# A fused attention and expert block: the second norm's shift moved into DRAM, the query constants and a transposition reordered

## The chip, the cores and the metric

The kernel runs on one core of a Trainium2 chip. The metric is the device time of one launch in microseconds; the time given for a kernel is the median over its runs.

## The reference

One adaptive-norm block over x of shape 4 x 2048 x 512 (8192 rows). Six modulation vectors per batch come from a conditioning input: shift, scale and gate for the attention (sa, ca, ga) and for the experts (sb, cb, gb).

```python
h = layernorm(x) * (1 + ca) + sa
x = x + ga * attention(h)          # segments of 128 rows, one head of width 512, plus a global part per segment
h = layernorm(x) * (1 + cb) + sb   # the second norm
x = x + gb * experts(h)            # top-1 routing to 16 experts, 512 slots each, 512 -> 2048 -> 512 with relu
```

The router takes softmax(h @ Wg + bg), the largest score of each row and its rank among the rows of the same expert; a row beyond slot 511 of its expert is dropped. In the attention the products of query and key are folded into one matrix (M = Wq' Wk), so a row's score has besides h M h' a constant per row, the query constant, that comes from the biases: the dot product of the normalised row with a vector vc per batch, plus a constant.

## The kernel before, in words

A prologue folds the weights and makes the modulation rows. Then 16 groups of 512 rows (four tiles of 128 rows, called segments here) run through a software pipeline, and at last 16 experts run one after the other. All fp32 products are made from a high and a low part in three matmuls (`split3`, L326 to L330).

In iteration i of the pipeline every engine's program (five programs, written out by hand and tied by semaphores) works on several groups at once: group i is projected (G tiles, U rows), group i-1 has its softmax and attention product, its residual and its second norm, group i-2 has its normalised rows h2 transposed for the router, and group i-3 is routed and scattered into the slot table. Each engine works strictly in the order of its own program.

TensorE (L687 to L775), for group i: G tile 0, transposes of the logit parts, G tile 1, transposes of h2 of group i-2 (L715), G tile 2, transposes of prob of group i-1 (L726), G tile 3, the attention product of group i-1 (L744, which reads pt_hi, pt_lo, u_hi, u_lo), U of group i (L754), the router's logit parts of group i-2 (L761), the transposes of the normalised rows xn of group i+1 (`transpose_xn`, L598), and the scores of group i (L773). The PSUM banks 0 to 3 (`big`) are used again and again: the transposes of xn for k = 0, 1, 2 write the banks from which VectorE takes u_lo(0), u_lo(1), u_lo(2), and wait for the semaphore u_split (L596); the scores go to bank 3 and wait for u_lo(3) (L770).

VectorE (L1339 to L1402): the softmax constants of group i-1, the router's logits, the probabilities, the statistics of the first norm of group i+1 (`stats1`), pt_lo (L1364), the router's slots (`route_slots`), h and the residual xr of group i-1 (L1377, L1381), the statistics of the second norm, then for group i the low parts u_lo (L1399) of the four U tiles. Between the second and the third of these stands `query_const` (L1265): four scalar_tensor_tensor instructions (L1271), one per segment, which multiply the rows of x with vc and sum them up, and a small one (L1275). Their elementwise result goes to `qc_junk`, which lies over the tile `prob`. Then come the low parts ht_lo of group i+1 (L1217).

ScalarE (L1001 to L1060): the exponentials, gt (`add_u`, L965), h2t (L1034, a Copy out of PSUM), pt_hi (L1039), u_hi(0) to u_hi(2) (L1009), the normalised rows of segments 0 to 2 of group i-1 (`normalise2`, L1016), u_hi(3), segment 3, then `modulate` for group i+1 (L957) and the logit parts (L1013).

GpSimd (L1594 to L1616): `normalise1` of group i+1 (L1558, L1561, four L1568), the scatter of group i-3 into the slot table (four indirect DMAs, L1590), the inverse root of the second norm, and then for each segment of group i-1 the product with 1 + cb (L1611) and the sum with sb (L1615), both in place in h2. For the last group VectorE does this for three of the segments (L1388 to L1393).

SP (L434 to L454) issues the loads and stores: x of group i+2, the global rows, xr of group i (a second load of x), then for group i-1 the store of the residual (L452), and the store of h2 into the DRAM tensor h_rows (L454), from which the experts later gather their rows. It waits for the semaphore before each of them, and everything behind it in the queue waits too.

```python
for s in range(GS):
    if s == 2:
        query_const(i)
    dve.wait_ge(u_hi_done, 4 * n + s + 1)
    dve.tensor_tensor(u_lo[:, s, :], big[s][:, :], u_hi[:, s, :].bitcast(F32), ALU.subtract) \
        .then_inc(u_split, 1)
```

Of the kernel before, what the change touches and what calls it, by code (L numbers as in the profile page):

```python
# [60 lines left out]
def build_block(nc, x, wq, bq, wk, bk, wv, bv, wo, bo, wg, bg, w1, b1, w2, b2, cond, wmod, out):  # L61
# [90 lines left out]
    bk_cols = keep("bk_cols", [P, KC, NBATCH], F32)  # L152
    q_const = keep("q_const", [P, 4], F32)
# [26 lines left out]
    logit_parts, = over(cursor[0], ("logit_parts", [P, ROWS], F32))  # L180
# [28 lines left out]
    qc_junk = prob[:].rearrange("p s t -> p (s t)")  # L209
# [32 lines left out]
    def sem(name):  # L242
# [35 lines left out]
    x2_ready, ln2_step, ln2_ready, ln2_rstd, xn2_done, h2_scaled, h2_ready = (sem(k) for k in (  # L278
        "x2_ready", "ln2_step", "ln2_ready", "ln2_rstd", "xn2_done", "h2_scaled", "h2_ready"))
    last_scaled = sem("last_scaled")  # L280
    x2_stored = [sem(f"x2_stored{i}") for i in range(2)]
    h2_stored = [sem(f"h2_stored{i}") for i in range(2)]
# [36 lines left out]
    def batch_of(g):  # L319
        return g.n // GPB  # L320

    def t1_bank(g, k):

        return t1_last if k == KC - 1 and not (isinstance(g.n, int) and g.n == 0) else big[k]

    def split3(pe, o, a_hi, a_lo, b_hi, b_lo, start, stop):  # L326
# [9 lines left out]
    (MCH, SCT, BCOL, FIRST4, WOT, UCOL, MCOL, VCH, HGT, LATE4, GROWS, GGT, SG, BROW, PGT, TG, B1T,  # L336
     PRO_END) = (0, 4, 5, 6, 7, 11, 12, 13, 17, 18, 19, 20, 21, 22, 23, 24, 25, 26)
# [24 lines left out]
    def _(sp):  # L362
        def w_rows(w):
            return w.rearrange("(c p) n -> p c n", p=P)

        def group_rows(rows, g):
            return rows[bass.ds(g.n * ROWS, ROWS), :].rearrange("(s p) d -> p s d", p=P)
# [66 lines left out]
        def iteration(i, cur, prev, load2):  # L434
# [5 lines left out]
            if cur:  # L440
# [7 lines left out]
                sp.dma_start(xr[i.par][:], group_rows(x_rows, i)).then_inc(xr_in[i.par], 16)  # L448
            if prev:
# [3 lines left out]
                sp.wait_ge(h2_ready, 4 * g.n + 4)  # L453
                sp.dma_start(group_rows(h2_dram, g), h2[g.par][:]).then_inc(h2_stored[g.par], 16)  # L454
# [36 lines left out]
        sp.wait_ge(h2_ready, 4 * NG)  # L491
# [32 lines left out]
    def _(pe):  # L524
# [130 lines left out]
        g_tile(Group(0, 0), 3)  # L655
        pe.wait_ge(gsum_prob, 1)
# [30 lines left out]
        def iteration(i, cur, prev, prev2, nxt, prev3):  # L687
# [59 lines left out]
            if cur:  # L747
                for s in range(GS):
# [7 lines left out]
                    last.then_inc(u_full, 1)  # L756
            if prev2:
# [6 lines left out]
            if cur and not g_tiles:  # L764
                pe.wait_ge(pro_evac, PRO_END)
            if nxt:
                transpose_xn(i.plus(1), False)
# [151 lines left out]
    def _(act):  # L919
# [76 lines left out]
        add_u(Group(0, 0), 3)  # L996
        copy_out(PGT, pg_t[:], pro_bank(PGT)[0:NSEG, 0:NSEG])
# [3 lines left out]
        def iteration(i, cur, prev, prev2, nxt, prev3):  # L1001
# [51 lines left out]
            if cur:  # L1053
                empty_u(3)
            if prev:
                normalise2(3)
# [654 lines left out]
```

## Time and profile before

| | |
|---|---|
| median of 3 runs | 1887.14 us (1886.38 to 1889.94) |
| the profiled execution, its own time | 1889.13 us |
| its span in the profile | 1887.4 us |
| granted clock of TensorE, mean | 0.984 |
| TensorE matmul busy | 1796.1 us (95%) |
| VectorE busy | 1225.6 us (65%) |
| ScalarE busy | 822.7 us (44%) |
| GpSimd busy | 870.3 us (46%) |
| DMA | 270.77 MB, mean 143 GB/s |

The prologue lasts until about 90 us, the 16 groups until about 640 us, the routing of the last groups and the first gather until about 690 us, and the experts from there to the end. Busy time of TensorE is what its matmuls cover; a wait shows as idle time ahead of the instruction that had to wait, with the name of what ended it.

### The profile page before, as it was taken

The numbers are of one execution on the slowest core, as the hardware profiler recorded it, in microseconds if no ns is written. First come the engines' busy times: TensorE is split into PE (matmuls) and PEld (weight loads), VectorE is DVE, ScalarE is ACT, GpSimd is POOL, SyncE is SP. The second block draws the span as 40 slices with busy tenths as digits, with TensorE's granted clock in tenths as the row PEclk, the third lists the DMA queues.
The fourth block names the chain that finished last, engine by engine and source line by source line (L and its number), as shares of the span: only waits on it lengthen the run. The fifth ranks groups of instructions, "written<-read, shape, count | busy, mean of one in ns | idle before, by whom it ended". The sixth has DMA issues, their size and how long they took to land.

```text
span 1887.4 us, 28151 instructions
## 1 busy us (share of the span) xinstructions
PE 1796.1 (95%) x9137; PEld 1486.9 (79%) x9138; DVE 1225.6 (65%) x1882; ACT 822.7 (44%) x1322; POOL 870.3 (46%) x709
## 2 busy tenths in 40 slices
PE   8999999999999549999999999999998999999998
PEld 3677787787787437888888888888888988888886
DVE  4568888888887753556554554537658886455762
ACT  2544554544554322433433343335545564334541
POOL 2145655656665441334343432416636757233632
PEclk9999999999999879999999999999999999999999
DMA  8322432342242524343535434345545455434622
GB/s 276 140 92 90 138 131 90 119 149 89 103 166 89 178 68 160 130 142 125 190 134 180 146 123 144 116 157 190 175 142 205 164 210 182 155 123 156 215 88 67
DMA packets 137915, 270.77 MB, mean 143 GB/s; under 512 B 17633, under 2 KB 18221, under 8 KB 137862
## 3 DMA queue, kind: packets, MB, share of 16 engines
q1 hardware_dynamic: 115338, 221.27, 33.6%
q0 software_dynamic: 22528, 48.86, 8.1%
q8 instruction: 29, 0.48, 0.1%
q14 instruction: 20, 0.16, 0.0%
HBM read 237.71 MB, written 50.72 MB: 153 GB/s over the span
## 4 chain that ended last, share of the span: by engine, by line
PE 77%; DVE 14%; issue 4%; ACT 3%; DMA 1%; POOL 0%; DVEq 0%; POOLq 0%; ACTq 0%; SPq 0%
PE bank L328 23%; PE bank L330 23%; PE bank L329 23%; PE bank L773 3%; DVE prob L1271 2%; DVE h L1377 2%; DVE xr L1381 2%; DVE stats L1156 2%; PE bank L715 1%; DVE u_lo L1399 1%; PE bank L816 1%; PE bank L598 1%; PE bank L536 1%; PE bank L587 1%; DVE h_lo L1438 0%
## 5 line engine op out<-in xcount | busy, mean ns | idle before, releaser
L1438 DVE TENSOR_TENSOR h_lo<-h_f,h_hi 128x512 fp32r<-128x512 f32 x256 | 221.3, 885 | 363.4 <-ACT h_f L1090 363.2
L1089 ACT ACTIVATE h_hi<-bank,b_col 128x512 fp32r<-128x512 f32 x256 | 176.4, 689 | 599.6 <-PE bank L330 582.1
L328 PE MATMUL bank<-bt_hi,w_hi 128*128 128x512 f32 (+4 forms) x1024 | 360.3, 352 | 8.4 <-DVE w_lo L1409 5.6
L330 PE MATMUL bank<-bt_hi,w_lo 128*128 128x512 f32 (+4 forms) x1024 | 359.4, 351 | 0.0
L329 PE MATMUL bank<-bt_lo,w_hi 128*128 128x512 f32 (+4 forms) x1024 | 359.4, 351 | 0.0
L328 PE MATMUL bank<-w_hi,h_hi 128*128 128x512 f32 x832 | 326.9, 393 | 3.3 <-DVE h_lo L1438 2.5
L329 PE MATMUL bank<-w_lo,h_hi 128*128 128x512 f32 x832 | 325.4, 391 | 0.0
L330 PE MATMUL bank<-w_hi,h_lo 128*128 128x512 f32 x832 | 324.9, 391 | 0.0
L328 PEld LDWEIGHTS bank<-bt_hi,w_hi 128*128 128x128 f32 x1024 | 194.7, 190 | 33.6 <-issue 9.6
L329 PEld LDWEIGHTS bank<-bt_lo,w_hi 128*128 128x128 f32 x1024 | 194.7, 190 | 21.0
L330 PEld LDWEIGHTS bank<-bt_hi,w_lo 128*128 128x128 f32 x1024 | 194.7, 190 | 20.3
L1634 POOL DMA_INDIRECT gb_rows<-mod_rows,tok_g x64 | 79.5, 1243 | 277.4 <-DVE tok_g L1515 221.6
L328 PEld LDWEIGHTS bank<-w_hi,h_hi 128*128 128x128 f32 x832 | 157.0, 189 | 36.4 <-issue 5.0
L330 PEld LDWEIGHTS bank<-w_hi,h_lo 128*128 128x128 f32 x832 | 156.9, 189 | 33.0
L329 PEld LDWEIGHTS bank<-w_lo,h_hi 128*128 128x128 f32 x832 | 156.9, 189 | 31.2
L1634 POOL DMA_INDIRECT xh<-h_rows,tok_h x64 | 87.1, 1361 | 201.2 <-DVE tok_h L1497 177.8
L1430 DVE TENSOR_TENSOR w_lo<-raw,w_hi 128x2048 fp32r<-128x2048 f32 x64 | 153.1, 2393 | 41.0 <-ACT w_hi L1079 40.9
L1090 ACT ACTIVATE h_f<-bank,b_col 128x512 f32<-128x512 f32 x256 | 174.3, 681 | 0.0
L1409 DVE TENSOR_TENSOR w_lo<-raw,w_hi 128x2048 fp32r<-128x2048 f32 x64 | 152.8, 2388 | 2.2
L1660 POOL TENSOR_TENSOR yo<-yo,gb_rows 128x512 f32<-128x512 f32 x60 | 96.1, 1602 | 107.0 <-DVE yo L1459 105.6
L1079 ACT ACTIVATE w_hi<-raw 128x2048 fp32r<-128x2048 f32 x64 | 122.6, 1916 | 0.0
L1665 POOL DMA_INDIRECT out_dram<-yo,tok_x x64 | 79.8, 1247 | 80.7 <-POOL yo L1662 53.9
(265 smaller groups left out, 3220.4 us busy)
## 6 DMA issues: line engine op xcount, KB each, us to landing
raw<-in_L_ffn_W_dram SPq DMA_DIRECT2D x128, 1024.0 KB, 5.5
xa<-in_L_attn_x_dram SPq DMA_DIRECT2D x16, 1024.0 KB, 5.3
xr<-in_L_attn_x_dram SPq DMA_DIRECT2D x16, 1024.0 KB, 8.1
out_dram<-xr SPq DMA_DIRECT2D x16, 1024.0 KB, 10.2
h_rows<-h SPq DMA_DIRECT2D x16, 1024.0 KB, 4.3
b_bc<-in_L_ffn_b_dram SPq DMA_DIRECT2D x16, 256.0 KB, 6.2
wm_a<-in_L_wmod_dram SPq DMA_DIRECT2D x2, 1024.0 KB, 11.1
wm_b<-in_L_wmod_dram SPq DMA_DIRECT2D x2, 1024.0 KB, 11.2
```

What stands on the lines that cost most here:

```text
L328: pe.matmul(o, a_hi, b_hi, start=start, stop=False)
L329: pe.matmul(o, a_hi, b_lo, start=False, stop=False)
L330: return pe.matmul(o, a_lo, b_hi, start=False, stop=stop)
L1079: act.activation(w2_hi[b % 2][:], raw[2 * (b % 2) + 1][:], ACT.Copy).then_inc(w2_hi_done, 1)
L1089: act.activation(h1_hi[b % 2][:, j, :], h_bank[j][:, :], ACT.Relu, bias=bias)
L1090: act.activation(h1_f[:, j, :], h_bank[j][:, :], ACT.Relu, bias=bias).then_inc(relu_done, 1)
L1409: dve.tensor_tensor(w1_lo[b % 2][:], raw[2 * (b % 2)][:], w1_hi[b % 2][:].bitcast(F32), ALU.subtract) \
L1430: dve.tensor_tensor(w2_lo[b % 2][:], raw[2 * (b % 2) + 1][:], w2_hi[b % 2][:].bitcast(F32), ALU.subtract) \
L1438: dve.tensor_tensor(h1_lo[b % 2][:, j, :], h1_f[:, j, :], h1_hi[b % 2][:, j, :].bitcast(F32), ALU.subtract) \
L1634: pool.indirect_dma_start(out=rows[:, j, :], out_offset=None, in_=source, in_offset=bass.IndirectOffsetOnAxis(tokens[:, j:j + 1], 0), boun ...
L1660: pool.tensor_tensor(yo[:, j, :], yo[:, j, :], gb_rows[:, j, :], ALU.mult).then_inc(y_scaled, 1)
L1665: pool.indirect_dma_start(out=out_rows, out_offset=bass.IndirectOffsetOnAxis(tok_x[:, j:j + 1], 0), in_=yo[:, j, :], in_offset=None, bound ...
```

## The change

- The second norm's shift sb is no longer added by GpSimd (L1615) or VectorE (L1393). SP writes it into h_rows for each group, broadcast from the table `sb_tab`, after the load of xr; for group 0 it first waits for the three late tables. GpSimd then, when the four segments are scaled and that store has landed (new semaphores `shift_stored`), issues one DMA that adds h2 to what is in h_rows. SP's store of h2 and its wait for h2_ready go.
- The router needs the shifted rows, so ScalarE adds the shift as it evicts the transposed rows (Identity with a bias per partition, `sb_col`, instead of Copy). `sb_col` takes the place of sc_t in memory and is made in the prologue by four small transposes (SCOL) and one copy.
- On VectorE the query rows of segments 0 to 2 stand after `stats1` and ahead of pt_lo, that of segment 3 ahead of u_lo(0), and the small instruction L1275 behind u_lo(0). `qc_junk` has memory of its own.
- On TensorE `transpose_xn` stands ahead of the logit parts, directly after U.
- On ScalarE `modulate` of the next group stands ahead of `normalise2(3)`.

```diff
@@ sync @@
                 sp.dma_start(xr[i.par][:], group_rows(x_rows, i)).then_inc(xr_in[i.par], 16)
+
+                if isinstance(i.n, int) and i.n == 0:
+                    sp.wait_ge(late_tab_in, 48)
+                shift = sb_tab[:, bass.ds(batch_of(i), 1), :].to_broadcast([P, GS, D])
+                sp.dma_start(group_rows(h2_dram, i), shift).then_inc(shift_stored[i.par], 16)
...
                 sp.dma_start(group_rows(out_rows, g), xr[g.par][:]).then_inc(x2_stored[g.par], 16)
-                sp.wait_ge(h2_ready, 4 * g.n + 4)
-                sp.dma_start(group_rows(h2_dram, g), h2[g.par][:]).then_inc(h2_stored[g.par], 16)
...
-        sp.wait_ge(h2_ready, 4 * NG)
@@ tensor @@
         g_tile(Group(0, 0), 3)
+        bank_free(SCOL)
+        for k in range(KC):
+            last = pe.transpose(pro_bank(SCOL)[:, k * NBATCH:(k + 1) * NBATCH], modr[:, SB, chunk(k)],
+                                ident[0:NBATCH, 0:NBATCH])
+        product(SCOL, last)
...
                     last.then_inc(u_full, 1)
+            if cur and not g_tiles:
+                pe.wait_ge(pro_evac, PRO_END)
+            if nxt:
+                transpose_xn(i.plus(1), False)
             if prev2:
                 pe.wait_ge(h2t_done, 4 * p2.n + 4)
...
                 last.then_inc(parts_full, 1)
-            if cur and not g_tiles:
-                pe.wait_ge(pro_evac, PRO_END)
-            if nxt:
-                transpose_xn(i.plus(1), False)
@@ scalar @@
+        copy_out(SCOL, sb_col[:].rearrange("p k b -> p (k b)"), pro_bank(SCOL)[:, 0:KC * NBATCH])
...
-                    act.activation(h2t[:, k, :], big[(k + 2) % 4][:, :], ACT.Copy).then_inc(h2t_done, 1)
+                    act.activation(h2t[:, k, :], big[(k + 2) % 4][:, :], ACT.Identity,
+                                   bias=sb_col[:, k, bass.ds(batch_of(p2), 1)]).then_inc(h2t_done, 1)
...
+            if nxt:
+                modulate(i.plus(1))
             if prev:
                 normalise2(3)
-            if nxt:
-                modulate(i.plus(1))
@@ vector @@
             if nxt:
                 stats1(i.plus(1))
+            if cur:
+
+                for s in range(GS - 1):
+                    query_row(i, s)
...
-                    dve.tensor_tensor(rows, rows, cb_tab[:, batch_of(p1), :], ALU.mult).then_inc(last_scaled, 1)
-                    dve.wait_ge(last_scaled, s + 1)
-                    dve.tensor_tensor(rows, rows, sb_tab[:, batch_of(p1), :], ALU.add).then_inc(h2_ready, 1)
+                    dve.tensor_tensor(rows, rows, cb_tab[:, batch_of(p1), :], ALU.mult).then_inc(h2_ready, 1)
             if cur:
+                query_row(i, GS - 1)
                 for s in range(GS):
-                    if s == 2:
-                        query_const(i)
                     dve.wait_ge(u_hi_done, 4 * n + s + 1)
                     dve.tensor_tensor(u_lo[:, s, :], big[s][:, :], u_hi[:, s, :].bitcast(F32), ALU.subtract) \
                         .then_inc(u_split, 1)
+                    if s == 0:
+                        query_const(i)
@@ gpsimd @@
                     pool.tensor_tensor(rows, rows, cb_tab[:, bass.ds(b, 1), :].rearrange("p b d -> p (b d)"), ALU.mult) \
-                        .then_inc(h2_scaled, 1)
-                    pool.wait_ge(h2_scaled, 4 * p1.n + s + 1 - first_seg)
-                    stand_alone(pool, pool_passed)
-                    pool.tensor_tensor(rows, rows, sb_tab[:, bass.ds(b, 1), :].rearrange("p b d -> p (b d)"), ALU.add) \
                         .then_inc(h2_ready, 1)
+                pool.wait_ge(h2_ready, 4 * p1.n + 4)
+                pool.wait_ge(shift_stored[p1.par], 16 * (p1.half + 1))
+                stand_alone(pool, pool_passed)
+                pool.dma_start(group_rows(h2_dram, p1), h2[p1.par][:], accum_op=ALU.add).then_inc(h2_stored[p1.par], 16)
```

`query_row` is the body of the old `query_const` for one segment, and `query_const` keeps the small instruction alone.

## Rows read from the trace of the kernel before

**Rows 1.** Stages: us, PE, PEld, DVE, ACT, POOL busy, clock, DMA, GB/s.

```profile
197.00:589.00 392.00, 383.42 (x2134) 307.91 (x2133) 339.97 (x790) 194.28 (x380) 239.44 (x219) 1.00 0.35 121
690.00:1280.00 590.00, 586.54 (x2727) 499.46 (x2728) 304.66 (x285) 225.13 (x311) 200.10 (x158) 1.00 0.42 144
```

**Rows 2.** TensorE waits, 88 to 640 us: total us, times, longest us.

```profile
PE bank L598 <- DVE u_lo L1399: 9.0, 12, 1.2
PE bank L715 <- POOL h L1615: 2.4, 1, 2.4
PE bank L773 <- DVE u_lo L1399: 2.1, 1, 2.1
...
PE bank L328 <- DVE ht_lo L1217: 1.1, 2, 0.7
```

**Rows 3.** TensorE timeline: start us, us, what [idle before, what ended it].

```profile
228.67 1.09 PE L598 MATMUL bank<-ident,xa 128*128 128x128 f32 x8 [0.59 <-DVE u_lo L1399]
...
549.91 0.39 PE L330 MATMUL bank<-v_hi,ht_lo 128*128 128x512 f32 x1
...
551.22 1.09 PE L598 MATMUL bank<-ident,xa 128*128 128x128 f32 x8
552.89 1.09 PE L598 MATMUL bank<-ident,xa 128*128 128x128 f32 x8 [0.57 <-DVE u_lo L1399]
...
588.73 1.09 PE L598 MATMUL bank<-ident,xa 128*128 128x128 f32 x8 [0.60 <-DVE u_lo L1399]
```

**Rows 4.** Timeline of VectorE at the end of the same period.

```profile
549.38 1.69 DVE L1271 SCALAR_TENSOR_TENSOR prob<-xa,vc_tab 128x512 f32<-128x512 f32 x1
...
551.22 1.02 DVE L1275 TENSOR_SCALAR per_tok<-per_tok,qc_bc 128x4 f32<-128x4 f32 x1
552.15 1.28 DVE L1399 TENSOR_TENSOR u_lo<-bank,u_hi 128x512 fp32r<-128x512 f32 x2
```

**Rows 5.** Timeline of all engines around pt_lo in that period.

```profile
531.15 0.16 DVE L1163 TENSOR_SCALAR per_tok<-mv 128x4 f32<-128x4 f32 x1
...
531.39 1.02 POOL L1558 TENSOR_TENSOR per_tok<-per_tok,half_neg 128x4 f32<-128x4 f32 x1 [5.45 <-DVE per_tok L1163]
...
532.52 0.69 ACT L965 ACTIVATE gt<-bank,u_col 128x512 f32<-128x512 f32 x1 [2.08 <-PE bank L330]
...
532.90 3.06 POOL L1568 TENSOR_SCALAR xa<-xa,per_tok 128x512 f32<-128x512 f32 x4 [0.21 <-POOL per_tok L1561]
...
533.73 0.69 DVE L1364 TENSOR_TENSOR pt_lo<-bank,pt_hi 128x512 fp32r<-128x512 f32 x1 [2.42 <-ACT pt_hi L1039]
...
535.52 0.39 PE L328 MATMUL bank<-u_hi,pt_hi 128*128 128x512 f32 x1
```

**Rows 6.** Timeline of ScalarE, that period and group 15.

```profile
548.11 2.22 ACT L1016 ACTIVATE h<-xr,per_tok 128x512 f32<-128x512 f32 x3
...
621.93 0.60 ACT L1009 ACTIVATE u_hi<-bank 128x512 fp32r<-128x512 f32 x1
```

**Rows 7.** Timeline of VectorE at the start of a period.

```profile
518.57 4.76 DVE L1217 TENSOR_TENSOR ht_lo<-ht,ht_hi 128x512 fp32r<-128x512 f32 x3 [0.30 <-ACT ht L957]
```

**Rows 8.** One line's instructions, GpSimd's shift: ns min/median/max.

```profile
L1615 POOL TENSOR_TENSOR h<-h,sb_tab x61: 1261/1497/1783, 120.6 to 653.0; 128x512 f32<-128x512 f32 x61
```

**Rows 9.** Timeline of GpSimd, one DMA of the scatter.

```profile
542.58 1.02 POOL L1590 DMA_INDIRECT slot_table<-pay,slot_i  x1 [0.30 <-issue]
```

**Rows 10.** DMA issues: count, KB each, median us to landing.

```profile
h_rows<-h SPq DMA_DIRECT2D x16, 1024.0 KB, 4.3
```

**Rows 11.** Timeline of the last groups, all engines.

```profile
625.02 3.81 PE L773 MATMUL bank<-ht,gt 128*128 128x128 f32 x32 [2.13 <-DVE u_lo L1399]
...
651.23 1.60 POOL L1611 TENSOR_TENSOR h<-h,cb_tab 128x512 f32<-128x512 f32 x1 [3.14 <-ACT h L1016]
...
653.41 1.63 DVE L1393 TENSOR_TENSOR h<-h,sb_tab 128x512 f32<-128x512 f32 x1
```

**Rows 12.** Timeline of VectorE in group 0, beside normalise1.

```profile
84.80 1.14 DVE L1271 SCALAR_TENSOR_TENSOR prob<-xa,vc_tab 128x512 f32<-128x512 f32 x1
```

More of the change, by code:

```diff
@@ L152, in build_block @@
     bk_cols = keep("bk_cols", [P, KC, NBATCH], F32)
+    sb_col = sc_t
     q_const = keep("q_const", [P, 4], F32)
@@ L179, in build_block @@
     prob, pt_hi, pt_lo = over(r_p, ("prob", seg_sq, F32), ("pt_hi", seg_sq, F32R), ("pt_lo", seg_sq, F32R))
-    logit_parts, = over(cursor[0], ("logit_parts", [P, ROWS], F32))
+    logit_parts, qc_junk = over(cursor[0], ("logit_parts", [P, ROWS], F32), ("qc_junk", [P, D], F32))
     batch_rows = [P, NBATCH, D]
@@ L208, in build_block @@
     m_f.append(m_f3)
-    qc_junk = prob[:].rearrange("p s t -> p (s t)")
     QCS2 = [QC, QCS]
@@ L277, in build_block @@
         "pt_full", "pt_hi_done", "pt_split", "av_full", "av_taken"))
-    x2_ready, ln2_step, ln2_ready, ln2_rstd, xn2_done, h2_scaled, h2_ready = (sem(k) for k in (
-        "x2_ready", "ln2_step", "ln2_ready", "ln2_rstd", "xn2_done", "h2_scaled", "h2_ready"))
-    last_scaled = sem("last_scaled")
+    x2_ready, ln2_step, ln2_ready, ln2_rstd, xn2_done, h2_ready = (sem(k) for k in (
+        "x2_ready", "ln2_step", "ln2_ready", "ln2_rstd", "xn2_done", "h2_ready"))
     x2_stored = [sem(f"x2_stored{i}") for i in range(2)]
+    shift_stored = [sem(f"shift_stored{i}") for i in range(2)]
     h2_stored = [sem(f"h2_stored{i}") for i in range(2)]
@@ L320, in batch_of, with group_rows @@
         return g.n // GPB
+    def group_rows(rows, g):
+        return rows[bass.ds(g.n * ROWS, ROWS), :].rearrange("(s p) d -> p s d", p=P)
     def t1_bank(g, k):
@@ L330, in split3 @@
         return pe.matmul(o, a_lo, b_hi, start=False, stop=stop)
-    (MCH, SCT, BCOL, FIRST4, WOT, UCOL, MCOL, VCH, HGT, LATE4, GROWS, GGT, SG, BROW, PGT, TG, B1T,
-     PRO_END) = (0, 4, 5, 6, 7, 11, 12, 13, 17, 18, 19, 20, 21, 22, 23, 24, 25, 26)
+    (MCH, SCT, BCOL, FIRST4, WOT, UCOL, MCOL, VCH, HGT, LATE4, GROWS, GGT, SG, BROW, SCOL, PGT, TG,
+     B1T, PRO_END) = (0, 4, 5, 6, 7, 11, 12, 13, 17, 18, 19, 20, 21, 22, 23, 24, 25, 26, 27)
     def pro_bank(q):
@@ L364, in w_rows @@
             return w.rearrange("(c p) n -> p c n", p=P)
-        def group_rows(rows, g):
-            return rows[bass.ds(g.n * ROWS, ROWS), :].rearrange("(s p) d -> p s d", p=P)
         def load_x(g):
@@ L1263, in _, with query_row @@
         dve.wait_ge(made, POOL_MADE)
-        def query_const(g):
-            b = batch_of(g)
-            for s in range(GS):
-                if s > 0:
-                    dve.wait_ge(qc_raw, 4 * g.n + s)
-                dve.scalar_tensor_tensor(out=qc_junk, in0=xa[g.par][:, s, :], scalar=1.0,
-                                         in1=vc_tab[:, bass.ds(b, 1), :].rearrange("p b d -> p (b d)"), op0=ALU.mult,
-                                         op1=ALU.mult, accum_out=QRAW[:, s:s + 1]).then_inc(qc_raw, 1)
+        def query_row(g, s):
+            wait_past(dve, qc_raw, 4 * g.n + s)
+            dve.scalar_tensor_tensor(out=qc_junk[:], in0=xa[g.par][:, s, :], scalar=1.0,
+                                     in1=vc_tab[:, bass.ds(batch_of(g), 1), :].rearrange("p b d -> p (b d)"),
+                                     op0=ALU.mult, op1=ALU.mult, accum_out=QRAW[:, s:s + 1]).then_inc(qc_raw, 1)
+        def query_const(g):
             dve.wait_ge(qc_raw, 4 * g.n + 4)
-            dve.tensor_scalar(QCS2[g.par], QRAW, qc_bc[:, bass.ds(b, 1)], SCALE, ALU.add, ALU.mult) \
+            dve.tensor_scalar(QCS2[g.par], QRAW, qc_bc[:, bass.ds(batch_of(g), 1)], SCALE, ALU.add, ALU.mult) \
                 .then_inc(qc_ready, 1)
```

## The prediction

> **What bounds the kernel now.** I read the busy time by stage first, then TensorE's waits, then the timeline of one period. In the router-and-attention stage (197 to 589 us) TensorE is busy 383.4 of 392 us, VectorE 340.0 and GpSimd 239.4; in the first experts (690 to 1280 us) TensorE is busy 586.5 of 590 [rows 1]. So the experts, which the change does not touch, have nothing to give, and in the first stage there are only the seconds that TensorE stands still. The list of its waits names them: 9.0 us in 12 waits of the transposes of xn (L598) for VectorE's u_lo (L1399), 2.1 of the scores (L773) for the same, 2.4 of the transposes of h2 (L715) for GpSimd's shift (L1615), 1.1 of a first product for ht_lo [rows 2]. The clock is granted in full there (1.00) [rows 1], so nothing is to be had from it.
>
> How the 9.0 us come about is to be seen in one period. U ends at 550.14 (its last matmul starts at 549.91; they follow each other every 0.23 us), the partial logits of L761 take the time up to 551.22, where eight transposes begin, and the other eight start at 552.89 after 0.57 us of idling [rows 3]. They write bank 2, which u_lo(2) must have left. VectorE reaches it at 552.15, since between u_lo(1) and u_lo(2) stand the four query rows (the last of them takes 1.69 us instead of 0.69) and the small L1275 with 1.02 us [rows 4]. From pt_lo at 533.73 VectorE has had no pause worth the name; the pause lies ahead of it: 2.42 us, from the end of stats1 (531.31) to pt_hi [rows 5]. There are 12 such waits of up to 1.2 us [rows 2], one per period of 36.0 us (228.67 to 588.73 is ten periods [rows 3]).
>
> **The change part by part.**
> (a) Query rows 0 to 2 move ahead of pt_lo, and L1275 behind u_lo(0). Three rows at 0.73 us from start to start are 2.2 us, the pause is 2.42 [rows 5]. Cover: the pause. If it were gone, pt_lo has some 0.9 us to spare: it ends at 534.42, and the first attention product starts at 535.52, its weight load a little before [rows 5]. After statistics there remain: row 3 (0.73), u_lo(0) (0.68), L1275 (between 0.2 and the 1.02 of its row), u_lo(1), u_lo(2). Statistics end at about 546.0 (row 3's 549.38 [rows 4] less three rows of 0.73 and two u_lo of 0.6). That puts the end of u_lo(1) at about 549.3 and of u_lo(2) at 550.0 at the latest, instead of 552.8. TensorE, which now goes to the transposes directly after U (550.14), wants u_lo(2) 1.1 us later, after eight of them, at 551.3. The wait goes entirely.
>
> (b) The transposes go before L761. The work is the same; its order matters for what is late next. Scores need u_lo(3), which needs u_hi(3); ScalarE evicts that only after three rows of normalise2 (548.11 + 2.22 = 550.33) and 0.60 us of its own (as in group 15) [rows 6], so 550.93, and u_lo(3) ends at 551.7. Scores start at 550.14 + 2.18 (16 transposes, twice 1.09) + 1.08 (L761, from U's end to 551.22) = 553.4 [rows 3]. Margin 1.7 us. For the next group modulate starts at once, as normalise2(3) now stands behind it: ht_lo(0) is there about 3 us after U's end, wanted 6.8 us after it. Today the last three ht_lo take 4.76 us beside GpSimd's multiply and add [rows 7]; that gets better with fewer of them. So (a) and (b) together: -9.0 us, and of the 1.1 us for ht_lo in the second group all, since ScalarE reaches modulate one normalise2 (0.74) earlier: -1.1.
>
> (c) GpSimd's four adds of 1.50 us (median) go [rows 8]: 6.0 us per group, off the path except at the end. In their place it waits for the multiplies and the shift store, and issues a 1 MB accumulating store. The trace has no such store; the nearest row is an indirect one of 128 rows at 1.02 us [rows 9], so 512 rows lie between 1.0 and 4 x 1.3 = 5.3 us of issue. I take 5.3, as nearest by rows moved. Queued behind it: normalise1, scatter and the inverse root of the second norm. Cover: GpSimd idles (392 - 239.4) / 10.9 periods = 14.0 us per period [rows 1], and gets 6.0 more. Cost 0; it would begin to bind at 20 us an issue. Landing: unknown, between the 4.3 us of the plain store [rows 10] and several times that; the buffer is overwritten two groups later, some 50 us on, so 0.
>
> (d) SP: the shift store (16 x 1 MB) stands behind xr's load and before the out store, the h2 store leaves, and with it the wait for h2_ready, behind which the next x load was queued. The new wait for the three tables stands in group 0 ahead of the x load for group 3, which waits for transposes anyhow. About 34 MB more traffic in 530 us is 63 GB/s on top of 121, at a DMA share of 0.35 [rows 1]: 0.
>
> (e) h2t with a bias: Identity with a bias from PSUM takes 0.69 (L965) [rows 5] where a Copy takes 0.60 [rows 6], so up to +0.4 us on ScalarE for four. It stands before a wait of 2 us for the next tile: 0 in the loop, 0.4 once at the end, counted in (f).
>
> (f) The last groups, where TensorE waits for others. Group 15's scores wait 2.1 us for u_lo(3); u_hi(3) is out at 621.93 + 0.60 = 622.53 [rows 6], so they can start at about 623.3 instead of 625.02 [rows 11]: -1.7. The 2.4 us that L715 then waits for GpSimd's add [rows 2] mostly lie beside the softmax that starts from the same scores; bounds of the pair 0 and 4.5, I take 1.7. Then the scaling of group 15: three multiplies and adds on VectorE and one of each on GpSimd, alternating, end at 655.04 and TensorE stands idle for it. Without adds the last is GpSimd's multiply, 651.23 + 1.60 = 652.83: -2.2 [rows 11]. All that follows (router, slot table, first gather) hangs on it.
>
> (g) Prologue: four small transposes and a copy more, bound 0.7 us; against it, rows and normalise1 of group 1 collide less or more, bound 0.5. Net 0.
>
> Sum: 9.0 + 1.1 + 1.7 + 2.2 = 14.0 us. The profiled execution took 1889.13 (span 1887.4, 1.7 around it), so 1875.1 for it; it is 2.0 above the median of 1887.14. On the median: 1873.1.
>
> **Rivals.**
> 1. The query rows collide with GpSimd in their new place. For it: the rows read two tiles of SBUF, and beside normalise1 such a row took 1.14 us once, instead of 0.69 [rows 12]; in the pause stand L1558 (1.02 us) and the first of four steps of L1568 (3.06 / 4 = 0.77 each) [rows 5]. If row 1 waits for L1558 and row 2 for one L1568, pt_lo starts at about 535.4, 1.7 late, of which 0.9 is free; TensorE then stalls 0.1 to 0.8 us per period, say 0.5 x 13 = 6.5. Time 1879.6. Against it: three rows colliding by 0.45 each would cost 1.35, half a microsecond beyond the margin at most.
> The Trainium skill (SBUF — State Buffer, Who interferes with whom) says that a VectorE instruction with two SBUF inputs contends with a GpSimd instruction that reads SBUF, and that whoever comes first holds the shared pair for its whole instruction; by that rule this rival is the expected course, and the row of 1.69 us agrees with it.
> 2. The same place, but at today's worst price: a row beside GpSimd costs 1.8 us (the last one does today, 1.69). Three are 5.4 in a pause of 2.4, so pt_lo is 3.0 late, 2.1 beyond its margin, against 0.8 saved: +1.3 x 13 = 17 us, less 5.0 of the other terms: slower, 1899. It decides from 1.7 us of delay per period on. Against it: 1.69 belongs to a two-input instruction of 1.3 to 1.7 us on GpSimd, and here stand ones of 0.77 and 1.02.
> 3. The wait only changes its place: scores wait for u_lo(3) (ScalarE late through the inverse root, or GpSimd held by the accumulating store), or the transposes still wait. Then of 14.0 only (f) and a little more is left: about 5, 1882. Margins of 1.3 and 1.7 us speak against it.
>
> **Numbers.** Forecast 0.62, rival 1 0.20, rival 3 0.11, rival 2 0.07. A difference within 0.2% (3.8 us) can't be told from none. Forecast, rival 1 and half or more of rival 3 are faster: 0.86; the rest of 3: 0.07; rival 2: 0.07. Range: below, the pair in (f) at 4.5 and 1 us elsewhere (18 saved, 1869); above, rival 1 and most of 3, 1882.
>
> **What the profile after would show.** Waits of L598 for u_lo gone, and none of L773, L328 for pt_lo or for h (L1377) in their place; the period 35.2 us (36.0 - 0.8); VectorE's pause before pt_lo under 0.5 us; ht_lo nearer 0.7 than today's 4.76 / 3 = 1.6; GpSimd's DMA issue of at most 5 us; first gather about 14 us earlier; experts unchanged from there. It is wrong if the rows before pt_lo span over 3.3 us, if GpSimd's issue reaches 15 us or more, or if the experts' part changes by more than 2 us.

## The result and the profile after

The changed kernel takes 1865.41 us (median of 5 runs, 1863.25 to 1868.66), the kernel before beside it 1889.65 (5 runs, 1886.38 to 1890.42). The ratio is 0.9875, 95% interval 0.9863 to 0.9886: 24 us less, where 14 were forecast, and below the range's lower end of 1869. The profiled execution took 1863.25 us; its span is 1861.6, against 1887.4 before. It is the fastest of the five, 2.2 us below their median, so what the trace gains (25.8 us) is a little more than what the medians do (24.2).

The stages after, in the columns of [rows 1], each shifted by what had been gained by then:

```profile
190.00:573.00 383.00, 383.00 (x2142) 311.88 (x2151) 300.73 (x791) 199.49 (x383) 192.00 (x187) 1.00 0.55 155
672.00:1262.00 590.00, 589.87 (x2756) 503.30 (x2755) 309.09 (x287) 230.68 (x317) 205.56 (x160) 1.00 0.42 145
```

In the attention loop TensorE never stands still in the records any more (383.00 of 383). The second line answers to the second of [rows 1]: TensorE is busy 589.87 us where it had been busy 586.54. That stage was to have nothing to give. It gave, and this is the largest part of the miss.

TensorE's waits after, 88 to 640 us, beside [rows 2]:

```profile
PE bank L723 <- POOL h L1624: 10.2, 1, 10.2
PE bank L723 <- ACT prob L1031: 1.8, 1, 1.8
PE bank L332 <- DVE pt_lo L1378: 1.7, 1, 1.7
...
PE bank L781 <- DVE u_lo L1410: 0.5, 1, 0.5
```

The 12 waits of the transposes for u_lo are gone, and so are those for ht_lo. What is left lies in the last two groups. The 10.2 is the pause ahead of the last h2 transposes, which in the kernel before (12.7 us for L1393) fell just behind 640 us. The scores of group 15 wait 0.5 instead of 2.1.

Two periods of TensorE's timeline, beside [rows 3]:

```profile
500.52 1.91 PE L601 MATMUL bank<-ident,xa 128*128 128x128 f32 x16
502.36 1.07 PE L773 MATMUL bank<-h2t,wg_s 128*32 128x512 f32 x8
503.35 3.84 PE L781 MATMUL bank<-ht,gt 128*128 128x128 f32 x32
...
535.54 1.91 PE L601 MATMUL bank<-ident,xa 128*128 128x128 f32 x16
```

The period is 35.02 us here. The sixteen transposes now run as one block, and the scores follow the logit parts without a gap.

VectorE and GpSimd ahead of pt_lo, beside [rows 5]:

```profile
516.25 0.17 DVE L1173 TENSOR_SCALAR per_tok<-mv 128x4 f32<-128x4 f32 x1
516.36 0.69 DVE L1278 SCALAR_TENSOR_TENSOR qc_junk<-xa,vc_tab 128x512 f32<-128x512 f32 x1
516.50 1.43 POOL L1571 TENSOR_TENSOR per_tok<-per_tok,half_neg 128x4 f32<-128x4 f32 x1 [5.25 <-DVE per_tok L1173]
...
517.09 0.69 DVE L1278 SCALAR_TENSOR_TENSOR qc_junk<-xa,vc_tab 128x512 f32<-128x512 f32 x1
...
517.83 0.69 DVE L1278 SCALAR_TENSOR_TENSOR qc_junk<-xa,vc_tab 128x512 f32<-128x512 f32 x1
518.01 0.56 POOL L1574 TENSOR_TENSOR per_tok<-per_tok 128x4 f32<-128x4 f32 x1
...
519.13 0.69 DVE L1378 TENSOR_TENSOR pt_lo<-bank,pt_hi 128x512 fp32r<-128x512 f32 x1 [0.61 <-ACT pt_hi L1049]
```

Each query row keeps its 0.69 us and pt_lo still has 0.61 us of pause before it. The collision costs GpSimd instead: its small L1571 takes 1.43 where it took 1.02 [rows 5], and nobody waits for that. The Trainium skill (SBUF — State Buffer, Who interferes with whom) has a VectorE instruction with two SBUF inputs contend with a GpSimd instruction that reads SBUF, and says that the order of issue decides who blocks. The trace agrees for the first row: it starts at 516.36 and keeps its time, GpSimd's instruction starts at 516.50 and loses. The second row does not fit so simply: it starts at 517.09, while L1571 is still running (until 517.93), and keeps its 0.69 us all the same.

The new store (one line's instructions, ns min/median/max) and the DMA issues (us from issue to landing):

```profile
L1629 POOL DMA_DIRECT2D h_rows<-h x16: 1361/1431/1571, 126.2 to 635.5; - x16
```

```profile
h_rows<-h POOLq DMA_DIRECT2D x16, 1024.0 KB, 9.5
```

Issuing costs GpSimd 1.43 us for 512 rows, near the lower bound of 1.0 from [rows 9] and far from the 5.3 taken. It lands after 9.5 us, the plain store of [rows 10] after 4.3.

**Where the time went.** Landmarks of TensorE in the two profiled executions: first scores 90.39 and 87.56 us, those of group 3 193.79 and 188.11, of group 14 589.66 and 573.40, of group 15 625.02 and 607.26; last h2 transposes 655.10 and 634.18; first gathered rows 685.86 and 665.57; the next expert's 768.59 and 743.76; end of span 1887.4 and 1861.6. The differences between successive marks are the gain by stage:

| Stage | gain, us | forecast |
|---|---|---|
| prologue | 2.8 | 0 |
| groups 0 to 14 (14 periods) | 2.9 + 10.6 = 13.4 | 10.1 |
| group 15, tail, router | 1.5 + 3.2 - 0.6 = 4.0 | 3.9 |
| first expert | 4.5 | 0 |
| all other experts | 1.0 | 0 |
| sum | 25.8 | 14.0 |

(The sum is that of the unrounded marks.) So three things want an explanation: 3.3 us more in the loop, 4.5 in the first expert, and 2.8 in the prologue.

### The profile page after: what moved, and what is told of

Same layout as the page of the kernel before. It is cut to its first block, busy times and chain, and to the rows that moved or that the text cites. A ratio compares the mean times of both kernels' runs of the same rounds, so it can differ in the third digit from the quotient of the medians.

```text
span 1861.6 us, 28129 instructions
## 1 busy us (share of the span) xinstructions
PE 1787.6 (96%) x9125; PEld 1486.2 (80%) x9142; DVE 1170.0 (63%) x1879; ACT 828.2 (44%) x1323; POOL 803.4 (43%) x664
## 3 DMA queue, kind: packets, MB, share of 16 engines
HBM read 237.71 MB, written 67.49 MB: 164 GB/s over the span
## 4 chain that ended last, share of the span: by engine, by line
PE 91%; DVE 2%; issue 2%; ACT 2%; POOL 1%; DMA 1%; POOLq 0%; DVEq 0%; ACTq 0%; SPq 0%
PE bank L332 27%; PE bank L334 26%; PE bank L333 26%; PE bank L781 3%; PE bank L723 2%; PE bank L601 1%; PE bank L824 1%; PE bank L590 1%; PE bank L539 1%; PE bank L773 1%; PE bank L753 1%; POOL yo L1675 0%; DMA out_dram<-yo,tok_x 0%; DVE h_lo L1451 0%; PE bank L734 0%
## 5 line engine op out<-in xcount | busy, mean ns | idle before, releaser
L334 PEld LDWEIGHTS bank<-w_hi,h_lo 128*128 128x128 f32 x832 | 156.4, 188 | 32.9
L1571 POOL TENSOR_TENSOR per_tok<-per_tok,half_neg 128x4 f32<-128x4 f32 (+1 forms) x33 | 45.6, 1382 | 167.3 <-DVE per_tok L1173 167.3
## 6 DMA issues: line engine op xcount, KB each, us to landing
wm_a<-in_L_wmod_dram SPq DMA_DIRECT2D x2, 1024.0 KB, 10.6
```

The costliest lines, as they stand in the source:

```text
L334: return pe.matmul(o, a_lo, b_hi, start=False, stop=stop)
```

## The experiments

There were ten runs, each with the kernel before beside it on the same chip; c1 and c6 repeat the two kernels, the other eight are new ones. To tell the parts apart they are called rows (VectorE's query rows and L1275 moved), transposes (ahead of the logit parts), modulation (ahead of the last normalisation) and shift (added in DRAM). The period is the distance between the scores of group 3 and group 14, divided by 11. c5 and c10 follow further down.

| Kernel | rows | transp. | modul. | shift | us | ratio (95%) | period |
|---|---|---|---|---|---|---|---|
| c1 | - | - | - | - | 1888.99 | 1.0005 (0.9995 to 1.0014) | 35.97 |
| c8 | yes | - | - | - | 1894.82 | 1.0028 (1.0018 to 1.0038) | 36.12 |
| c2 | yes | yes | yes | - | 1884.29 | 0.9979 (0.9970 to 0.9988) | 35.71 |
| c3 | - | - | - | yes | 1878.03 | 0.9938 (0.9925 to 0.9952) | 35.58 |
| c4 | - | yes | yes | yes | 1890.60 | 1.0014 (1.0005 to 1.0023) | 36.58 |
| c9 | yes | - | - | yes | 1867.53 | 0.9886 (0.9867 to 0.9906) | 34.97 |
| c7 | yes | - | yes | yes | 1865.94 | 0.9877 (0.9862 to 0.9891) | 34.97 |
| c6 | yes | yes | yes | yes | 1867.04 | 0.9883 (0.9869 to 0.9897) | 35.03 |

### c1, the kernel before again

No edit; a second trace of it.

> The kernel before, unchanged, for a second trace. Theory: 24 us of difference are 14 of the predicted terms plus three stretches that the prediction put at nothing: the prologue (2.8 us shorter in the changed kernel's trace, with the same instructions up to 48 us), the loop (0.2 us per period more than the idle times listed), and the first expert (TensorE waits 2.5 us at 715 us and then runs 3.4 us at the lower clock level). If prologue and first expert belong to the program, this trace shows again TensorE's first product at 16.6 us, the first xn transposes of group 1 at 88.6 and the wait of 2.5 us near 715. If they are chance, at least one of them is gone and the span is 2 to 5 us shorter or the run differs by that much. Ratio 1.000.

The time and the waits are those of before, and the 2.5 us stall in the first expert is there again. It belongs to the kernel and not to the one execution.

### c2, the three reorders without the shift

```diff
 # before, with the query rows, transpose_xn and modulate placed as in the change
 # kept: GpSimd's and VectorE's additions of sb_tab, SP's store of h2
```

> The kernel before with the three reorders alone (query rows, transposes of xn ahead of the logit parts, modulate ahead of the last normalised segment); the shift stays an add on GpSimd. Theory (the order was the bound): the loop's period falls to 35.0 to 35.1 us, no wait of L598 for u_lo is left, 11 to 13 us saved in the loop, total gain 13 to 18 us (ratio 0.990 to 0.993). Rival (GpSimd's adds, by holding up VectorE, made the wait): ht_lo stays at 1.6 us, a wait for ht_lo or the scores appears and the period stays above 35.5; gain under 8 us.

4 us, not the 13 to 18 that theory had. The wait of the transposes for u_lo is gone; in its place the products wait for ht_lo (TensorE's waits, 88 to 640 us):

```profile
PE bank L327 <- DVE ht_lo L1216: 4.9, 9, 0.7
```

All four ht_lo of a group now run beside GpSimd's multiplies and adds, and their median is 1.76 us where it had been 1.37 (192 to 586 us here, 197 to 589 before). So rival 3 is what the reorders do alone.

### c3, the shift alone

```diff
 # the change, with rows, transpose_xn and modulate back where they were before
```

> The changed kernel with the three reorders taken back: only the shift goes over DRAM. Theory: the waits of L598 stay (8 to 9 us, period 35.8 to 36.0), the gain is the tail's, 4 to 6 us, plus what the first expert's wait is worth if the program's layout decides it (4.5 us): ratio 0.9975, or 0.995 with it. Rival (relief of GpSimd is worth most): period under 35.5 and a gain over 10 us.

The shift alone brings 12 us by the ratio, 4 of them by a cause that c5 shows. Neither theory held whole: the gain is the rival's (over 10), the period of 35.58 lies between the two. Removing half of GpSimd's long instructions quickens VectorE: the median ht_lo is 0.69 us where it had been 1.37. The wait for u_lo stays in part:

```profile
PE bank L601 <- DVE u_lo L1407: 5.0, 8, 0.7
PE bank L781 <- DVE u_lo L1407: 2.1, 1, 2.1
```

This trace has periods with the wait and periods without it, and so shows what a wait costs beside its idle time (TensorE's timeline):

```profile
189.97 1.97 PE L601 MATMUL bank<-ident,xa 128*128 128x128 f32 x16
191.77 1.50 PE L781 MATMUL bank<-ht,gt 128*128 128x128 f32 x12
...
330.73 1.09 PE L601 MATMUL bank<-ident,xa 128*128 128x128 f32 x8
332.39 1.09 PE L601 MATMUL bank<-ident,xa 128*128 128x128 f32 x8 [0.57 <-DVE u_lo L1407]
333.32 0.94 PE L781 MATMUL bank<-ht,gt 128*128 128x128 f32 x7
```

From the first transpose to the scores it is 1.80 us in one go, and 2.59 with the wait. Of the 0.79 between them, 0.57 is idle; 0.22 is not listed anywhere.

### c4, all but the query rows

```diff
-            if cur:
-
-                for s in range(GS - 1):
-                    query_row(i, s)
...
-                query_row(i, GS - 1)
                 for s in range(GS):
+                    if s == 2:
+                        query_const(i)
```

> The changed kernel with the query rows back between u_lo(1) and u_lo(2); transposes of xn and modulate stay in their new places. Theory: since the transposes now come 1.1 us earlier and want u_lo(2) all the same, they wait longer: 1.6 to 2.3 us per period, period 36.0 again or worse, total 5 us of gain or less against before. Rival (the transposes' place was the cure, the rows' place does nothing): period 35.0 to 35.2, gain over 18 us.

Slower than before, by 2.6 us, although the first expert's stall (c5, below) is gone here too. The theory held. TensorE's timeline and VectorE's:

```profile
483.78 1.09 PE L601 MATMUL bank<-ident,xa 128*128 128x128 f32 x8 [1.69 <-DVE u_lo L1407]
...
520.82 1.09 PE L601 MATMUL bank<-ident,xa 128*128 128x128 f32 x8 [1.80 <-DVE u_lo L1407]
```

```profile
517.37 1.66 DVE L1281 SCALAR_TENSOR_TENSOR qc_junk<-xa,vc_tab 128x512 f32<-128x512 f32 x1
...
519.18 1.00 DVE L1285 TENSOR_SCALAR per_tok<-per_tok,qc_bc 128x4 f32<-128x4 f32 x1
520.09 1.28 DVE L1407 TENSOR_TENSOR u_lo<-bank,u_hi 128x512 fp32r<-128x512 f32 x2
```

The fourth row and the small instruction behind it are as slow as before, and u_lo(2) as late. But the transposes now come directly after U, and the 1.07 us of logit parts that had covered that much of the lateness stand behind them. Hence waits of 1.7 to 1.8 us in eight of the groups, where c3 has 0.6 to 0.7, and a period 1.0 longer than in c3. Moving the transposes forward is no gain by itself; it takes a cover away.

### c9 and c7, which parts are needed

```diff
 # c7: the change, with transpose_xn back behind the logit parts
 # c9: c7, and modulate(i.plus(1)) back behind normalise2(3)
```

> The changed kernel with TensorE's eight transposes of the next stripe's normalised rows back behind the logit parts, in two fours as before; query rows, modulation and the shift in DRAM stay changed. Theory A (nothing waits for u_lo any longer, so the place of the transposes is free but for one more drain of TensorE in each group): period 35.03 to 35.3, whole 1865 to 1869. Theory B (the transposes ahead cover the wait for ht_lo and u_lo's end; behind, each group waits again): period 35.4 to 35.9, whole 1870 to 1876.

> The changed kernel with the transposes back behind the logit parts and the modulation back behind the last stripe's normalisation: of the change only the moved query rows and the shift in DRAM are left. Theory A (these two are the whole gain and only together, since the shift's GpSimd additions no longer stand beside the rows; the other two reorders are free): period 35.0 to 35.1, no wait for u_lo, waits for ht_lo under 1 us in all, whole 1865 to 1868. Theory B (the modulation ahead of the normalisation is what keeps ht_lo early now): waits for ht_lo of 0.3 to 0.7 us in each group again, period 35.4 to 35.9, whole 1871 to 1880.

(The expectation for c7 speaks of eight transposes in two fours; the trace shows sixteen, which in the kernel before ran as two runs of eight.) Theory A holds in both; the periods lie a little below what it gave. With rows and shift alone no wait for u_lo or ht_lo is left between 188 and 600 us, and the period is 34.97:

```profile
187.94 1.06 PE L769 MATMUL bank<-h2t,wg_s 128*32 128x512 f32 x8
188.94 1.97 PE L601 MATMUL bank<-ident,xa 128*128 128x128 f32 x16
190.74 2.51 PE L781 MATMUL bank<-ht,gt 128*128 128x128 f32 x21
```

The other two reorders bring nothing that can be measured: the intervals of c6, c7 and c9 overlap.

### c8, the query rows alone

```diff
+                for s in range(GS - 1):
+                    query_row(i, s)
...
-                    if s == 2:
-                        query_const(i)
```

> The kernel before with only the query constants' rows moved behind pt_lo; shift still added on GpSimd, transposes and modulation where they were. Theory A (the rows between the two low halves are what made u_lo(2) late, so the move alone brings what the loop can give while GpSimd's long chain sets the rest): wait for u_lo under 2 us in all, period 35.6 to 35.8, whole 1882 to 1886. Theory B (the rows now stand beside GpSimd's additions of the shift, which are slowed and make ht_lo late): period 36.0 or more, whole 1888 to 1892.

(The rows moved ahead of pt_lo, not behind it as the expectation says.) The numbers of theory B, and worse than it said: 5 us slower than before. The waits for u_lo are gone from the loop, and more time goes to ht_lo:

```profile
PE bank L327 <- DVE ht_lo L1216: 11.5, 19, 0.7
PE bank L714 <- POOL h L1619: 3.9, 1, 3.9
```

One period of c8, TensorE, VectorE and GpSimd:

```profile
517.76 1.97 PE L597 MATMUL bank<-ident,xa 128*128 128x128 f32 x16
519.56 3.74 PE L772 MATMUL bank<-ht,gt 128*128 128x128 f32 x32
...
521.45 4.60 DVE L1216 TENSOR_TENSOR ht_lo<-ht,ht_hi 128x512 fp32r<-128x512 f32 x3 [0.47 <-ACT ht L956]
522.08 1.73 POOL L1615 TENSOR_TENSOR h<-h,cb_tab 128x512 f32<-128x512 f32 x1
526.10 0.50 PE L327 MATMUL bank<-ht_hi,m_hi 128*128 128x512 f32 x1 [0.70 <-DVE ht_lo L1216]
```

and the same place in the kernel before, which goes with [rows 7]:

```profile
514.88 1.09 PE L598 MATMUL bank<-ident,xa 128*128 128x128 f32 x8
517.13 1.09 PE L598 MATMUL bank<-ident,xa 128*128 128x128 f32 x8 [1.16 <-DVE u_lo L1399]
518.06 3.74 PE L773 MATMUL bank<-ht,gt 128*128 128x128 f32 x32
519.36 1.72 POOL L1611 TENSOR_TENSOR h<-h,cb_tab 128x512 f32<-128x512 f32 x1
```

Count both from the first transpose. The three ht_lo start after 3.69 us in both and take 4.60 here and 4.76 before; GpSimd's multiply beside them starts after 4.32 and 4.48. They stand where they stood. What moved is TensorE: its scores start after 1.80 us instead of 3.18, so it comes that much sooner to the products that want ht_lo, and waits there. The wait for u_lo had covered the lateness of ht_lo, which was there all along and which goes with GpSimd's adds (c3). So theory B's mechanism, that the moved rows bring it about, is not what the traces show, or only in part: the median ht_lo of the loop is 1.58 us, against 1.37 before. The period grows by 0.13 us (1.4 in all); another 2.8 lies between the scores of group 15 and the last h2 transposes (626.74 to 659.66, 32.9 us, before 30.1), 1.1 in the router and 1.9 in the first expert, by TensorE's clock (below).

### c5 and c10, the stall in the first expert

TensorE stood 2.48 us in the first expert of the kernel before, and then worked on at the lower clock. Its timeline:

```profile
712.26 0.39 PE L330 MATMUL bank<-bt_hi,w_lo 128*128 128x512 f32 x1
...
715.12 0.49 PE L328 MATMUL bank<-w_hi,h_hi 128*128 128x512 f32 x1 [2.48 <-DVE h_lo L1438]
...
717.00 0.63 PE L328 MATMUL bank<-w_hi,h_hi 128*128 128x512 f32 x1
717.42 0.63 PE L329 MATMUL bank<-w_lo,h_hi 128*128 128x512 f32 x1
```

By the code this product waits for one h_lo and one w_lo that were both done before 712; the h_lo that the view names is only the latest event it could find. The DMA queues of one microsecond, 712 to 713, of the same execution:

```profile
DMA packets 197, 0.40 MB, mean 401 GB/s; under 512 B 8, under 2 KB 8, under 8 KB 196
...
q1 hardware_dynamic: 196, 0.39, 100.5%
q8 instruction: 1, 0.02, 6.8%
```

A packet of instructions arrives while the loads of w1 and w2 (issued at 707.31 and 707.72) fill every DMA engine; between 700 and 712 there had been none. The changed kernel, c3 and c4 have no such stall, and all three have the four small transposes of the prologue (SCOL) in TensorE's program, which with their weight loads are eight instructions. c5 adds these and their copy to the kernel before, and nothing else; c10 issues the transposes twice.

```diff
         g_tile(Group(0, 0), 3)
+        bank_free(SCOL)
+        for k in range(KC):        # c10: for k in [*range(KC), *range(KC)]
+            last = pe.transpose(pro_bank(SCOL)[:, k * NBATCH:(k + 1) * NBATCH], modr[:, SB, chunk(k)],
+                                ident[0:NBATCH, 0:NBATCH])
+        product(SCOL, last)
@@ scalar @@
+        copy_out(SCOL, sc_t[:].rearrange("p k b -> p (k b)"), pro_bank(SCOL)[:, 0:KC * NBATCH])
```

> The kernel before, with only the prologue's transposition of the second norm's scale into a column (8 small TensorE transposes and a ScalarE copy) added, whose result nothing reads. It is there for the 2.48 us in which TensorE stood at 712.6 to 715.1 in the first expert, ahead of the low halves' products and with nothing that the code makes it wait for, followed by products at half clock. Theory D (the stall comes of the load of w1 and w2 that lands at that time, or of h_lo): it stays at 2.3 to 2.6 us and the whole is 1889 +- 1.5. In both, loop period 36.0 and the wait for u_lo(2) as before.

> The kernel before with the eight added small transposes of the prologue issued twice, so that TensorE's program ahead of the first expert is longer by sixteen instructions instead of eight. Theory L (the stall in the first expert comes when a piece of TensorE's program is fetched while the load of w1 and w2 fills the DMA engines; the packet of the instruction queue came at 712 to 713 before and at 708 to 710 with eight more instructions, ahead of the load): a packet still earlier or the next one clear of the load, so no stall of over 1 us there, whole 1885 to 1888, unless another piece now meets another load. Theory D (the eight helped by chance of the run): the 2.3 to 2.6 us stall is back, whole 1889 +- 1.5.

(Where the expectations say eight transposes, the trace shows four and four weight loads in c5, eight and eight in c10; what they transpose is the second norm's shift, not its scale.) c5 takes 1885.62 us, ratio 0.9978 (0.9969 to 0.9988); c10 1885.35, ratio 0.9980 (0.9971 to 0.9990). More work, nothing of it used, and 4 us less. In c5's trace the loop is as before (waits for u_lo 9.6 us in 12), and the stall is gone: TensorE is busy 12.00 of the 12 us from 710 to 722. One packet has moved ahead of the load, which is issued at 710.07 here. The DMA queues of 708 to 710, where nothing else is under way:

```profile
DMA packets 1, 0.02 MB, mean 8 GB/s; under 512 B 0, under 2 KB 0, under 8 KB 0
...
q8 instruction: 1, 0.02, 3.4%
```

The packets of the instruction queue (q8) in all traces, as the microsecond in which they come, counted from the issue of that load:

| Kernel | load issued | packets | stall |
|---|---|---|---|
| before | 707.31 | -13, -9, +5, +8 | 2.48 |
| c1 | 707.17 | -13, -9, +5, +8 | 2.47 |
| c2 | 704.52 | -14, -10, +4, +7 | 2.25 |
| c8 | 714.83 | -13, -9, +4, +8 | 2.52 |
| c5 | 710.07 | -14, -9, -1, +6 | none |
| c10 | 705.03 | -15, -9, -1, +5 | none |
| c3 | 700.13 | -15, -9, -1, +5 | none |
| c4 | 714.02 | -14, -9, -1, +6 | none |
| after, c7 | 686.90, 686.79 | -14, -9, -1, +6 or +5 | none |
| c6, c9 | 687.31, 689.33 | -14, -9, 0, +6 | none |

Read in steps of 0.1 us, the packet in question comes 4.8 to 5.1 us behind the load's issue in the four kernels that stall, and between 0.7 us ahead of it and 0.4 behind in the others. A packet that comes in the midst of the load is no harm by itself (the next one, +5 or +6, of the kernels that do not stall). The eight instructions are four products with their weight loads, and four products are 0.9 us at 0.23 each: by this estimate a fetch that falls at the load's issue with them falls some 0.9 us behind it without them.

The stall's size by the timeline: 2.48 us of standing, and eight products at 0.43 us from start to start (717.00 to 717.42) instead of 0.23, another 1.6. Together 4.1, where c5 gains 4.2 by its ratio. The stage itself, from the first gathered rows to the next expert's, sorts the traces by two things, the stall and the time when the clock comes back after the long pause ahead of the gather:

| First expert's stage, us | clock back within 4 us | clock back after 8 to 9.5 us |
|---|---|---|
| with the stall | 82.7 (before), 83.3 (c1), 83.1 (c2) | 84.7 (c8) |
| without it | 78.2 (after), 78.4 (c6), 78.3 (c7), 78.5 (c9), 78.2 (c10) | 80.5 (c3), 80.4 (c4), 80.4 (c5) |

By the means of the cells the stall is worth 4.7 us in the first column and 4.2 in the second; the late clock is worth some 2 more. It hides half of c5's gain in c5's own trace (80.4 against 82.7).

The Trainium skill (Advanced Engine Details and Errata, ISA Cache) gives instruction caches with lines of 16 KB, 256 instructions each, 32 KB in all and 128 KB on TensorE. The page of the profile agrees in the size of a line: 29 packets with 0.48 MB are 16.6 KB each. That packet and stall move together is shown; that the packet was a line of TensorE's program, asked for while straight code ran and late behind a full load, is argued, since no view names the engine of a packet.

### c6, the changed kernel again

> The changed kernel once more, unchanged, for a second trace. If the 2.3 us by which the products of the prologue were quicker in its first trace (L539, 15.4 us where the other kernels have 16.4 to 17.0) belong to the run and not to the change, the first scores begin at 90 +- 1 us here and the profiled execution takes 1865 to 1867; if they belong to the change, 87.5 to 88 again. Whole: 1865.5 +- 1.5, ratio 0.987 to 0.989. Loop period 35.03, no stall of over 1 us in the first expert.

1867.04 us with the same period. Its first scores begin at 87.72 us, so the quicker prologue stands in both traces of the changed kernel. But it is not the change's work. The slice of 33 to 36 us, after (c6 and c7 are like it; columns of [rows 1]):

```profile
33.00:36.00 3.00, 3.00 (x7) 1.29 (x6) 0.00 (x0) 0.33 (x1) 0.00 (x0) 0.74 1.05 389
```

and in c10, which is the kernel before but for eight small transposes:

```profile
33.00:36.00 3.00, 3.00 (x7) 1.27 (x6) 0.00 (x0) 0.35 (x1) 0.00 (x0) 0.74 1.05 384
```

c9, which has the change's rows and shift, is like the kernel before:

```profile
33.00:36.00 3.00, 3.00 (x4) 1.04 (x4) 0.00 (x0) 0.00 (x0) 0.00 (x0) 0.50 1.05 382
```

The same products find a clock of 0.74 in the one kind of prologue and 0.50 in the other, and the granted clock is back at 1.00 at 35 us or only at 37 to 38. The kind goes neither with the rows (c9 against c7) nor with the shift (c10 against c3). It may not even go with the kernel: c10's trace is the fastest of its twelve executions, 4.5 us below their median, as those of the changed kernel and of c6 and c7 are the fastest of theirs, and no trace shows the others. What decides it stays open, and so does how much of the 2.8 us lies in the median.

## Why the prediction was wrong

**Direction and place were right, and the mechanism in part; the size was not.** By its own steps:

- *(a) and (b), 9.0 + 1.1 us*: measured 13.4 over 14 periods. The period went from 35.99 to 35.03; it was to be 35.2. The idle time that the records show was counted rightly (twelve waits of 0.43 to 1.16), but a wait costs TensorE more than its idle row. In the kernel before, transposes and wait take 2.60 us from 551.22 to the scores at 553.82, of which 0.57 is idle, so 2.03 for two blocks of eight; as one block they take 1.84 (500.52 to 502.36). That is 0.19 us for each of the 12 waits, 2.3 of the missing 3.3, and c3 shows the same within one trace (0.22). With it the loop from group 3 to 14 comes out: 8.6 of idle and 11 times 0.19 are 10.7, measured 10.6. The other 1.0 lies in the first three groups, and no run takes it apart. The failed step is the reading of the term's size as the sum in the list of waits.
- *(b), the transposes ahead of the logit parts*: no gain (c7), and a loss of 1.0 us per period where the rows stay (c4). The margin of the scores behind u_lo(3) held (1.3 us in the period above, where 1.7 was worked out).
- *Modulation ahead of the normalisation, part of the 1.1*: nothing by itself (c9). ht_lo came in time because GpSimd's adds went; its mean fell from 1281 ns (L1217, x42) to 813 (L1227, x43).
- *(c), the adds "off the path except at the end"*: the failed sentence with most weight for the mechanism. The instructions that left GpSimd slowed VectorE's ht_lo, and once u_lo was in time this was the next limit (c2, c8). The prediction counted GpSimd's work by GpSimd's path alone. It expected quicker ht_lo "with fewer of them", but put no price on it. For the loop this did no harm to the sum, by luck: the change makes both parts at once.
- *Issue and landing of the store*: 1.43 us, inside 1.0 to 5.3, and 9.5 us of landing, without cost, as expected.
- *(d)*: the load on the DMA engines rose from 121 to 155 GB/s, a little over half the 63 more that were reckoned, and no wait for it appears. The pages of the profile count 16.8 MB more written (50.72 and 67.49) and none more read, where 34 were taken. *(e)*: 0.69 us each, as forecast. Whether it costs the router anything is not shown: from the last h2 transposes to the gathered rows it is 30.8 us before and 31.4 after, but also 31.4 in c5, which has no bias, and 30.7 in c4, which has it.
- *(f), 1.7 + 2.2*: measured 1.5 from group 14 to 15 and 3.2 from there to the last h2 transposes, less 0.6 in the router. The sum is right (4.0) in part by luck: the second term is 1.0 too small, and the router's loss takes most of that back.
- *(g), 0*: measured 2.8 in the traces, by a cause outside the change, open in its origin.
- *"The experts have nothing to give"*: wrong by 4.5 us in the first of them, and beyond the 2 us that the prediction had itself named as a sign of being wrong. 586.54 of 590 busy [rows 1] was taken for full; its missing 3.5 us were one stall of 2.48 and 1.0 elsewhere, and the lower clock behind the stall does not show as idle. The change removed the stall by eight instructions in its prologue that lie ahead in the program, not by what it does to the groups. Without it the change would have brought about 20 us, by estimate (24 less the 4 of c5 and c10).
- *Rival 1 and 2* (rows collide in the new place): GpSimd pays, not VectorE. *Rival 3* (the wait changes place): is what happens without the shift (c2), though not because something else became late: ht_lo was as late before, hidden behind the wait for u_lo (c8). The change escapes it only by its two main parts together: rows alone +5 us, shift alone -12, both -22 (c9); the last two contain the 4 us of the stall.

The range failed at its lower end because it held no term for anything outside the edited stages: the experts' 4.5 us were put at nothing from their busy share, and the loop's waits were priced 3.3 us too low.

## What to carry to other kernels

The list of waits is a lower bound: each wait of TensorE between two blocks of transposes cost a further 0.2 us here. What an engine's long SBUF instructions cost must also be read from its neighbour's durations. And a wait can hide another lateness behind it, which comes out when the first is cured. A stall that no semaphore in the code explains, in straight code beside a large load, may hang on where the program's pieces are fetched; a few unused instructions ahead of it show whether it does, and a change should not be credited with it. Test reorders together and apart: of four, two carried everything, and one of these two alone made the kernel slower.

## What was not expected of the hardware

- Four unused transposes of the prologue (eight instructions) make the kernel 4 us faster, while a 16 KB packet of instructions moves from 5 us behind the issue of a 2 MB load to just ahead of it.
- The clock after a pause comes back at different times in executions of nearly the same program. In the kernel before TensorE stood still for 12.7 us up to 655 us, and again for 19.2 up to 686. There the slices of 685 to 690 and 690 to 695 us show a clock of 0.62 and 1.00; in c5 both show 0.50, after nearly the same pause (18.9), and the first expert's stage takes some 2 us more where the clock is that late. Runs of c5 lie between 1880.74 us, at a mean granted clock of 0.987, and 1887.94, at 0.981. The Trainium skill (TensorE: Matmul & The Clock Gate, What's actually happening) says that the number of matmuls at the lower clock varies from run to run of one kernel; these runs agree.
- Where the first of the query rows and GpSimd's small L1571 overlap, GpSimd's, which starts later, takes 1.43 instead of 1.02 us, and the row keeps 0.69. Where GpSimd's long multiply starts first, as in c4, the row takes 1.66 to 1.81.
- An accumulating 1 MB store costs GpSimd 1.43 us of issue and takes 9.5 us to land.
